# Delta rule preparation: two scalings of 128x4096 made by GpSimd instead of VectorE

## The reference

```python
def step(S, inp):
    qt, kt, vt, at, gkt = inp
    Sp = S * jnp.exp(gkt)[..., None]
    u = jnp.einsum('bhk,bhkv->bhv', at, Sp) + vt
    S = Sp + jnp.einsum('bhk,bhv->bhkv', kt, u)
    o = jnp.einsum('bhk,bhkv->bhv', qt, S)
    return (S, o)
...
q = silu(x @ Wq)
k = silu(x @ Wk)
v = silu(x @ Wv)
log_f = jax.nn.log_sigmoid(x @ Wf)
gamma = -jax.nn.sigmoid(x @ Wgamma)
...
k = l2norm(k.reshape(b, n, H, HD))
gk = jnp.broadcast_to(log_f[..., None], (b, n, H, HD))
a = k * gamma[..., None] * jnp.exp(gk)
out = dplr_delta_rule(q, k, v, a, gk)
```

## Time and profile before

| | before |
|---|---|
| runs | 1333.67, 1330.51, 1326.14 us |
| median | 1330.51 us |
| the profiled execution, its own time | 1334.64 us |
| its span, first to last instruction | 1332.8 us |
| PE busy | 912.9 us (68%) |
| DVE busy | 793.4 us (60%) |
| ACT busy | 551.8 us (41%) |
| POOL busy | 578.7 us (43%) |
| mean granted TensorE clock | 0.874 of full speed |

### The profile page before, as it was taken

One profiled execution on the slowest core, in us unless ns is written; L12 is line 12 of the kernel. 1 busy time (PEld: TensorE's weight loads), 2 busy tenths in 40 slices (PEclk: granted clock), 3 DMA queues, 4 the chain that ended last, 5 costly groups with the idle time before them and its releaser, 6 DMA issues. The chain is left out here.

```text
span 1332.8 us, 25209 instructions
## 1 busy us (share of the span) xinstructions
PE 912.9 (68%) x8236; PEld 629.3 (47%) x8236; DVE 793.4 (60%) x1615; ACT 551.8 (41%) x1205; POOL 578.7 (43%) x659
## 2 busy tenths in 40 slices
PE   0678878788787785029982958984676773507993
PEld 0355544545455462017771328734555563206772
DVE  6366676667676676202226129999999999501223
ACT  1465756566475652014431631015555541103441
POOL 3347467273655731444441000007777780172442
PEclk9989999899999996559995969996889887758997
DMA  2312303033040304036642680000001001016665
GB/s 69 126 65 65 128 3 128 18 112 112 19 128 7 122 3 192 32 96 181 185 137 76 205 205 1 1 0 0 0 0 63 16 16 32 9 52 164 183 188 166
DMA packets 129403, 110.08 MB, mean 83 GB/s; under 512 B 21984, under 2 KB 115104, under 8 KB 128928
## 3 DMA queue, kind: packets, MB, share of 16 engines
q1 hardware_dynamic: 123760, 98.08, 25.4%
q0 software_dynamic: 5120, 10.53, 2.4%
q10 hardware_dynamic: 432, 0.20, 0.1%
HBM read 64.01 MB, written 44.65 MB: 82 GB/s over the span
## 5 line engine op out<-in xcount | busy, mean ns | idle before, releaser
L583 DVE TENSOR_SCALAR a_mag<-a_pS 128x1024 int32<-128x1024 int32 (+1 forms) x192 | 182.1, 955 | 130.5 <-PE a_pS L767 128.7
L271 POOL TENSOR_TENSOR a_pw<-a_pw,a_decay 128x128 f32<-128x128 f32 (+1 forms) x192 | 121.3, 635 | 185.6 <-ACT a_pw L375 184.7
L375 ACT ACTIVATE a_pw<-a_mag,a_eps_a 128x1024 f32<-128x1024 f32 (+1 forms) x192 | 173.7, 928 | 64.7 <-DVE a_mag L583 63.8
L1053 POOL DMA_INDIRECT ys_dram<-f_yo,f_who x96 | 91.9, 957 | 139.3 <-DVE f_yo L1253 120.6
L1241 DVE TENSOR_SCALAR f_ysT<-f_bY,f_b2s 128x256 f32<-128x256 f32 x48 | 23.2, 484 | 175.1 <-PE f_bY L1341 147.3
L795 PE MATMUL a_pOff<-a_pw,a_vo 128*18 128x64 f32 x3584 | 126.5, 225 | 0.0
L1600 POOL TENSOR_TENSOR d_pb_p<-d_Q,d_s_sb 128x512 f32<-128x512 f32 x32 | 37.3, 1167 | 198.1 <-ACT d_s_sb L1700 198.1
L767 PE MATMUL a_pS<-a_qf,a_kf 128*128 128x128 bf16 (+7 forms) x512 | 98.4, 295 | 10.4 <-issue 6.8
L795 PEld LDWEIGHTS a_pOff<-a_pw,a_vo 128*18 128x18 f32 x3584 | 104.8, 102 | 0.0
L1096 ACT ACTIVATE f_hs<-f_bH,f_b1s 128x256 f32<-128x256 f32 x192 | 75.2, 474 | 67.1 <-issue 37.6
L1045 POOL DMA_INDIRECT xs_dram<-f_xa,f_pos x64 | 61.7, 964 | 94.0 <-DVE f_pos L1226 75.1
(11 more groups left out here) (333 smaller groups left out, 1897.3 us busy)
## 6 DMA issues: line engine op xcount, KB each, us to landing
parts_scratch<-a_parts SPq DMA_DIRECT2D x32, 384.0 KB, 4.0
f_w1s<-in_L_ffn_w_dram SPq DMA_DIRECT2D x48, 256.0 KB
f_w2s<-in_L_ffn_w_dram SPq DMA_DIRECT2D x48, 256.0 KB
a_kc<-parts_scratch SPq DMA_DIRECT2D x8, 1024.0 KB, 6.0
a_qf<-parts_scratch SPq DMA_DIRECT2D x8, 1024.0 KB, 9.0
xs_dram<-blank SPq DMA_DIRECT2D x12, 516.0 KB, 5.3
f_xs<-xs_dram SPq DMA_DIRECT2D x48, 129.0 KB, 2.2
parts_scratch<-a_parts SPq DMA_DIRECT2D x16, 256.0 KB, 4.0
```

Of the source, the lines that this page charges most:

```text
L271: pool.tensor_tensor(own, own, decay[:, k, m, pairs_of(hf, qs), :], ALU.mult)\
L375: act.activation(pw[:, n % 4, 0:N], mag[:, n % 3, 0:N], ACT.Square, bias=eps_a[:, 0:1])\
L583: dve.tensor_scalar(mag[:, n % 3, 0:2 * N].bitcast(I32).rearrange("p (l t) -> p l t", l=2), pS[:, 2 * (n % 2):2 * (n % 2) + 2, 0:N].bitcas ...
L1053: pool.indirect_dma_start(ys_dram[f][:, :], bass.IndirectOffsetOnAxis(ap=who[:, q, a:a + 1], axis=0), yo[:, q, a, :], None).then_inc(ys_ou ...
```

## The change

The two instructions L1831 and L1873 are taken out of VectorE's queue and put into GpSimd's, behind its constants. The key scaling waits for `decay_step` 14, the sums of squares and K; the query scaling waits for the key scaling (GpSimd's own order) and for 22 products. ScalarE waits for the key scaling (`cc_step` 5) before it writes sums into K. VectorE waits for it before L1897 of before, and for the query scaling (`cc_step` 6) before the chain starts.

```diff
@@ block.gpsimd
             pool.affine_select(out=ident[:, :], in_=ident[:, :], compare_op=ALU.not_equal, fill=1.0,
                                base=0, pattern=[[-1, P]], channel_multiplier=1).then_inc(s["c_consts"], 1)
 
+            pool.wait_ge(s["decay_step"], 7 + CH - 1)
+            pool.wait_ge(s["ksq_ps"], 1)
+            pool.wait_ge(k_in, k_in_0 + 48)
+            step(pool.tensor_tensor(W[:, :, :, :].rearrange("p d j c -> p d (j c)"),
+                                    K[:, :, :, :].rearrange("p d j c -> p d (j c)"),
+                                    beta[:, :].unsqueeze(1).broadcast_to([P, HD, T]), ALU.mult))
+            pool.wait_ge(s["prod_done"], KW_AT)
+            step(pool.tensor_tensor(Q[:, :, :, :], Q[:, :, :, :],
+                                    G[:, :, 0, :].unsqueeze(1).broadcast_to([P, HD, CH, NCH]), ALU.mult))
@@ block.scalar
             for i in range(CH - 1):
 
+                act.wait_ge(s["cc_step"], 5)
                 act.wait_ge(s["sums_done"], KW_AT + max(k for k, p in enumerate(KW) if p[0] == i) + 1)
@@ block.vector
             product(9)
-            dve.tensor_tensor(W[:, :, :, :].rearrange("p d j c -> p d (j c)"), K[:, :, :, :].rearrange("p d j c -> p d (j c)"),
-                              beta[:, :].unsqueeze(1).broadcast_to([P, HD, T]), ALU.mult).then_inc(s["w_step"], 1)
-            wn = 1
+            wn = 0
@@
             dve.wait_ge(s["prod_done"], KW_AT)
-            dve.tensor_tensor(Q[:, :, :, :], Q[:, :, :, :],
-                              G[:, :, 0, :].unsqueeze(1).broadcast_to([P, HD, CH, NCH]), ALU.mult)\
-                .then_inc(s["w_step"], 1)
-            wn += 1
@@
             dve.wait_ge(s["prod_done"], len(PIECES))
+            dve.wait_ge(s["cc_step"], 5)
             dve.tensor_tensor(K[:, :, CH - 1, :], K[:, :, CH - 1, :],
@@
+            dve.wait_ge(s["cc_step"], 6)
             dve.memset(c0[:, 0:HD * HD], 0.0).then_inc(s["w_step"], 1)
```

## The result

| | before | after |
|---|---|---|
| median | 1331.05 us (4 runs) | 1345.55 us (4 runs, 1341.6 to 1348.74) |
| ratio, 95% interval | | 1.0105, 1.0077 to 1.0132 |
| the profiled execution: own time, span | 1334.64, 1332.8 us | 1343.8, 1341.7 us |
| POOL busy | 578.7 us | 598.8 us |
| DVE busy | 793.4 us | 802.4 us |

What follows compares the result with a forecast made beforehand. VectorE was taken to bound the preparation from 813 to 899 us. Two scalings, each 8.8 us held off less 4.4 removed, plus 0.7 for TensorE's clock, gave +9.5 us: 1340.0 against the median 1330.51, range 1333.0 to 1346.0.

Steps and rivals of the forecast that it cites:

- What bounds: From beta written (813.4 us) to the preparation's end (899.3), VectorE sets the end; each microsecond there is one of the program.
- The sign: Whether GpSimd runs beside VectorE: no, they hold each other off and take turns, so both places get slower, +4.4 us each.
- GpSimd's price: Each of GpSimd's two 128x4096 multiplications takes 8.8 us, with bounds of 7.4 and 10.3 us.
- Place two: Query scaling: GpSimd's turn comes behind the first L1864, VectorE's queue waits 8.8 us, 4.4 removed: +4.4 us.
- TensorE's clock: TensorE, idle 7 to 9 us in both gaps, may fall to 1.2 GHz: +0.7 us, between 0 and 3.
- place one: Key scaling: GpSimd runs from 815.6 to 824.4 us, VectorE's L1827 stands 8.8 us, 4.4 removed: +4.4 us.
- the slack: After the query scaling, VectorE comes to each sum 3 to 5 us after TensorE has it, hiding nearly all clock loss.
- The sum: Whole program: 2 x (8.8 - 4.4) + 0.7 = +9.5 us, bounds +6.0 to +14.8.
- The gain without collision: Preparation: 8.8 us of VectorE work removed, less 1.3 us waiting for TensorE's piece 9 at L1841: 7.5 us gained.
- rival two: At both scalings the engines do not hold each other off: -7.5 us, 1323.0 us; chance 0.06.
- Rival one: VectorE's back-to-back instructions keep GpSimd out until PSUM readers L1841 and L1881: +2.9 us, 1333.4 us; chance 0.12.

Runs made afterwards that it cites:

- e3: Kernel before with both scalings left out, made by no engine (output not the reference's): ratio to before 0.9928, preparation stretch 77.28 us against 85.96.
- e8: Kernel before with both scalings moved to GpSimd in eight pieces each, nearly all in the chain, ScalarE first copying K and decays: ratio to before 0.9925.
- e1: The change with the query scaling put back to VectorE, so only keys are scaled on GpSimd: ratio to before 1.0053, preparation stretch 92.25 us against 85.96.
- e2: The change with the key scaling put back to VectorE, so only queries are scaled on GpSimd: ratio to before 1.0034, preparation stretch 90.44 us against 85.96.
- e4: The change with GpSimd's two multiplications replaced by memsets that write zeros and read nothing (output not the reference's): ratio to before 0.9952.
- e5: The change with two more GpSimd waits, so each scaling starts beside VectorE instructions that read PSUM (L1841, L1881): ratio to before 1.0042.
- e10: Only the key scaling on GpSimd, cut into eight instructions of 128x512, queries on VectorE: ratio to before 1.0053, preparation stretch 92.20 us against 85.96.
- e11: The change itself, unedited, measured again beside the kernel before on the same chip: 1345.42 against 1331.33 us, ratio 1.0104.
- e9: The change plus 9 needless matmuls filling TensorE's first gap before piece 9 of the sums: median 1341.31 us, ratio to before 1.0090.
- e7: Kernel before with only the query scaling moved to GpSimd in eight pieces, the first beside PSUM readers, the others in the chain: ratio to before 0.9970.
- e6: The change plus 18 needless matmuls in TensorE's first gap, a filler of 15.61 us against a gap of 8.6: ratio to before 1.0133.

## Why the prediction was right, and where its sizes were off

- **What bounds.** Right. VectorE without gaps between 813 and 899 us set the end of the preparation. What was taken from it or stood in its way came out in full (e3 and e8: -8.7; e1 and e2: +6.3 and +4.5), and the chain behind kept its length.
- **The sign.** Right, by the step that decided it: the short collisions of the earlier trace rows and the turns of the earlier trace rows hold for 8.7 us too (first L1838 8.85 us). e4 and e5 tell the multiplication from a memset and two SBUF inputs from one; e10 shows the turns. The signs that the prediction named are there too: two GpSimd instructions of 8.8 us (recorded with 10.92 and 9.08 us, their waits for VectorE included), TensorE idle for 8.58 and 7.55 us, and GpSimd's first product of the chain at 908.94 in a trace that has K 3.6 us earlier.
- **GpSimd's price.** 8.8 us each were taken from two cases of L271. They took 8.83 and 8.85 us with nothing in the way (e5), and held VectorE off for 8.6 us. Place two, +4.4 us in the sum, measured +4.3 (e2: +4.5, e11: +4.9). The estimate of 9.0 us from the GPSIMD Engine Reference of the Trainium skill (Performance versus the Vector engine) lies 0.2 us above the 8.83 us measured.
- **TensorE's clock.** The term that was too small. The mechanism was named, but priced at 0.7 us in all, with at most 1.5 us at place one, a bound given without its working. There it cost 1.92 us of waiting: VectorE was ready for the last two L1850 at 828.55, and piece 9, begun at 824.95, ended at 830.44, since it took 5.49 us at 0.50 of the clock; with the 2.87 us of full clock (e9) it would have ended at 827.8, in time. The same wait is in every profile with the key scaling at this place and no filler (1.92 us in after, e1 and e10, 1.75 in e11). At place two the time over e7's 39.46 us is 8.63 us in after, 8.82 in e2 and 9.27 in e11, against 8.63 us of holding off. So the slack hid the clock but for 0 to 0.6 us; in e11 a product waits 0.55 us for TensorE. In e5 the clock was 0.50 too behind 6.15 us of idling (824 to 829 us), and VectorE waited for nothing.
- **The sum.** +9.5 us forecast, +10.6 and +11.1 in the stretches, +14.5 and +14.1 in the medians. So the forecast was good for what it describes, the preparation, but that the median stayed in the range, by 0.45 us, is luck: it holds 3 to 4 us that no term of the sum describes. Where they lie is not shown: the profiles are single executions, the lower ends of both intervals (+10.2 and +10.9) lie just under the stretch, and the kernel before varies by 5 us outside the preparation from one profile to the other. Chance alone is not shown either. In all twelve comparisons with a changed kernel the difference of medians lies above that of the stretch, by 0.6 (e8) to 4.5 us (e6), also in e3, which only takes work out, while before against itself shows none. By the ratios it is less regular: e3 and e8 lie 0.8 and 1.2 us below their stretches, e2 at its own, the others above. That stays open.
- **The gain without collision** was put at 7.5 us, with 1.3 us given to TensorE. That step failed: piece 9's end was compared with the start of the ten L1841, while only the last two of them need it. The right figure is 8.7 us (e3). So rival two's time was 1.2 us too high; it did not occur.
- **Rival one** did not occur by itself. Made by hand (e5) its stretch was +3.7 us against +2.9 forecast: VectorE lost 6.6 and 5.8 us where 6.2 and 5.5 were put.

## What to carry to other kernels

Before moving elementwise work from VectorE to an idle GpSimd, look at what VectorE runs there: where its instructions had two SBUF inputs, the move cost GpSimd's longer time on VectorE's own path (8.6 us for 4.3 us removed); where they read one input from PSUM, or had one input only, for as long as GpSimd's instruction lasted, it cost nothing. Price what stands behind the standstill too, since an engine left idle for 8.6 us came back at half its clock. And the idle time worth looking for may be in another stage: in e8 fourteen of the sixteen pieces lie in the chain and cost nothing, while each of the two whole scalings in the preparation cost 4.5 to 6.3 us.

## What the runs showed that was not expected

- A VectorE copy of 128x512 from SBUF to SBUF was held by a GpSimd memset, 1.64 instead of 0.42 us, although the multiplications beside it ran on at full speed (e4), and the second memset beside it took 3.68 instead of 3.51 us.
- VectorE's record counts the time it is held off as busy: a multiplication of 64 elements with 8.85 us. A mean by line (seven instructions, 1.58 us each) would not show which one it was.
- TensorE's clock did not fall when zeros were multiplied in the gap (e9): needless work on an idle engine shortened the stretch by 2.0 us.
